# One GpSimd subtraction a step handed to VectorE in the first attention half of an attention-and-experts layer

## What is computed

```python
disp = (x @ W_disp).reshape(B, T, nh, bd).transpose(0, 2, 1, 3)      # 16 heads of 16
disp_win = _windows(disp, delta)                                     # the last 64 positions
strain = disp_win - disp[:, :, :, None, :]
bond_act = gelu(strain @ W_strain + rel_emb @ W_pos)
bond_logits = (bond_act @ W_bond)[..., 0]
damage_act = gelu(strain @ W_dmg + b_dmg)
damage = sigmoid((damage_act @ W_dmg_out)[..., 0] + b_dmg_out[0])
logits = bond_logits - 10.0 * damage
weights = softmax(where(cmask, logits, -inf))                        # over the 64 positions
out = einsum('bntd,bntde->bnte', weights, val_win) ... @ W_cproj
```

## Time and profile before

| | |
|---|---|
| time, median of 3 runs | 3710.76 us (3703.95 to 3714.79) |
| the profiled execution | 3708.35 us, its span 3706.8 us |
| busy over the span | DVE 77%, ACT 67%, PE 67%, POOL 63%, PEld 33% |
| first attention half, 350 to 1660 us | ACT 1096.7, DVE 1090.1, POOL 1022.6, PE 890.8 us busy |

### The profile page before, as it was taken

One profiled execution on the slowest core, in us unless ns is written; L12 is line 12 of the kernel. 1 busy time (PEld: TensorE's weight loads), 2 busy tenths in 40 slices (PEclk: granted clock), 3 DMA queues, 4 the chain that ended last, 5 costly groups with the idle time before them and its releaser, 6 DMA issues. The chain is left out here.

```text
span 3706.8 us, 64220 instructions
## 1 busy us (share of the span) xinstructions
PE 2501.0 (67%) x21226; PEld 1211.9 (33%) x21226; DVE 2861.7 (77%) x4254; ACT 2500.9 (67%) x1716; POOL 2327.2 (63%) x1604
## 2 busy tenths in 40 slices
PE   4662666776676766767888885566666676667666
PEld 2441112222222222246666661122222222222224
DVE  6888988888888888822433337999999899989981
ACT  1111979988888888843333337878878877778883
POOL 1222888678787878823343437777777777667771
PEclk9886879888888898868999997878778877878885
DMA  6773122222222222226878872222222222222222
GB/s 247 284 277 129 38 78 84 90 88 85 68 86 86 84 97 76 77 89 195 243 243 244 242 241 74 70 78 73 81 70 84 71 82 76 75 82 78 77 69 88
DMA packets 366243, 435.33 MB, mean 117 GB/s; under 512 B 48673, under 2 KB 282993, under 8 KB 366066
## 3 DMA queue, kind: packets, MB, share of 16 engines
q1 hardware_dynamic: 284658, 278.53, 24.0%
q0 software_dynamic: 57216, 143.22, 11.6%
q10 hardware_dynamic: 24192, 11.02, 1.1%
HBM read 233.83 MB, written 198.77 MB: 117 GB/s over the span
## 5 line engine op out<-in xcount | busy, mean ns | idle before, releaser
L1069 DVE SCALAR_TENSOR_TENSOR u_dve<-s_win,rpos,ps_here 128x512 f32<-128x512 f32 x1792 | 1197.6, 740 | 213.4 <-PE ps_l L1153 107.6
L1153 PE MATMUL ps_l<-u_dve,wsel 128*32 128x512 f32 x6144 | 984.8, 770 | 392.6 <-ACT u_dve L993 186.1
L927 POOL TENSOR_TENSOR u_pool<-s_win 128x4096 f32<-128x4096 f32 x128 | 1021.7, 7982 | 7.5 <-DMA s_win<-s_dram 5.3
L993 ACT ACTIVATE u_dve<-u_dve 128x4096 f32<-128x4096 f32 x224 | 809.9, 3616 | 56.8 <-DVE u_dve L1069 56.7
L1064 DVE TENSOR_TENSOR u_dve<-s_win,ps_here 128x4096 f32<-128x4096 f32 x160 | 703.3, 4412 | 43.1 <-PE ps_l L1153 43.1
L915 POOL DMA_INDIRECT yg<-yslot_dram,slot_now x512 | 485.6, 948 | 285.7 <-issue 148.5
L906 POOL DMA_INDIRECT xslot_dram<-xr,slot_now x512 | 494.6, 966 | 147.0 <-issue 143.6
L991 ACT ACTIVATE u_pool<-u_pool,bdmg_sb 128x4096 f32<-128x4096 f32 x128 | 474.5, 3707 | 66.1 <-POOL u_pool L927 66.1
L991 ACT ACTIVATE u_dve<-u_dve,bdmg_sb 128x4096 f32<-128x4096 f32 x128 | 474.4, 3706 | 15.8 <-DVE u_dve L1064 15.5
L1153 PEld LDWEIGHTS ps_l<-u_dve,wsel 128*32 128x32 f32 x6144 | 194.8, 128 | 842.8 <-issue 549.8
L1014 ACT ACTIVATE at_sb<-ps_u 128x512 f32<-128x512 f32 x256 | 151.0, 590 | 375.3 <-PE ps_u L1216 301.7
(11 more groups left out here) (142 smaller groups left out, 3011.1 us busy)
## 6 DMA issues: line engine op xcount, KB each, us to landing
band<-band_dram SPq DMA_DIRECT2D x32, 2048.0 KB
xslot_dram<-zero SPq DMA_DIRECT2D x16, 2688.0 KB, 9.1
xs<-xslot_dram SPq DMA_DIRECT2D x168, 256.0 KB, 3.6
yslot_dram<-ys POOLq DMA_DIRECT2D x168, 256.0 KB, 3.2
band_dram<-ml SPq DMA_DIRECT2D x64, 512.0 KB
we<-in_w_expert SPq DMA_DIRECT2D x336, 64.0 KB, 2.8
s_win<-s_dram SPq DMA_DIRECT2D x64, 288.0 KB, 5.9
s_dram<-s_sb POOLq DMA_DIRECT2D x16, 1024.0 KB, 4.7
```

Of the source, the lines that this page charges most:

```text
L927: pool.tensor_tensor(item_buffer(n), windows(par, ty, d0, 8), s_win[:, par, ty, PAD:PAD + TC].unsqueeze(1).to_broadcast([P, 8, TC]), ALU.s ...
L993: act.activation(u, u, ACT.Gelu).then_inc(gelu_done, 1)
L1069: last = dve.scalar_tensor_tensor(out=item_buffer(n)[:, d, :], in0=s_win[:, par, ty, d0 + d + 1:d0 + d + 1 + TC], scalar=rpos[:, d0 + d:d0 ...
L1153: last = pe.matmul(ps_l[32 * g:32 * g + 32, cgrp % 2, ty, :], wsel[:, ty, q, :], item_buffer(n)[:, d, :], start=(q == 0), stop=(q == 3))
```

## The change

In the first half VectorE subtracts the item n = 15 as well, 13 items a step, and GpSimd three (3, 7 and 11). The buffer of item 15 stays the one of `u_pool` in which GpSimd wrote it. The second half keeps its 12 and 4. The two semaphores' counts differ between the halves now, so that every wait on them in the second half is shifted by what the first left over (`D0`, `P0`). The subtraction of item 15 is the form that VectorE uses for `ty` 1 already (L1064), and it reads `ps_here`.

```diff
-            NP = len(on_pool)
-            dve_of = [sum(q % 4 not in on_pool for q in range(n + 1)) for n in range(NI)]
+            by_pool = ((3, 7, 11), (3, 7, 11, 15))[half]
+            dve_of = [sum(q not in by_pool for q in range(n + 1)) for n in range(NI)]
+            D0, P0 = ((0, 0), (first, -first))[half]
...
-                    return u_pool[:, (pool_of[n] - 1) % 2]
+                    return u_pool[:, n // 4 % 2]
...
-                    return n + 1 - 8 // NP
+                    return n - 7
...
-                            if "i" in st and n % 4 in on_pool:
+                            if "i" in st and n in by_pool:
                                 if pool_of[n] == 1:
                                     pool.wait_ge(win_loaded[par], 32 * it + 32)
...
-                                if n % 4 in on_pool:
-                                    if some(NPI * s + pool_of[n]):
-                                        act.wait_ge(sub_pool, NPI * s + pool_of[n])
+                                if n in by_pool:
+                                    if some(NPI * s + P0 + pool_of[n]):
+                                        act.wait_ge(sub_pool, NPI * s + P0 + pool_of[n])
...
-                            if "i" in st and n % 4 not in on_pool:
+                            if "i" in st and n not in by_pool:
...
-                        if some(ND * s):
-                            pe.wait_ge(sub_dve, ND * s)
+                        if some(ND * s + D0):
+                            pe.wait_ge(sub_dve, ND * s + D0)
```

More of the change, by code:

```diff
@@ L742, in load_windows @@
                         if some(it):
-                            if some(ND * (2 * it + par - 1)):
-                                sp.wait_ge(sub_dve, ND * (2 * it + par - 1))
+                            if some(ND * (2 * it + par - 1) + D0):
+                                sp.wait_ge(sub_dve, ND * (2 * it + par - 1) + D0)
                                 sp.sem_inc(held, 1)
-                            if some(NPI * (2 * it + par - 1)):
-                                sp.wait_ge(sub_pool, NPI * (2 * it + par - 1))
+                            if some(NPI * (2 * it + par - 1) + P0):
+                                sp.wait_ge(sub_pool, NPI * (2 * it + par - 1) + P0)
                                 sp.sem_inc(held, 1)
@@ L977, in step @@
                             if "i" in st:
-                                if n % 4 in on_pool:
-                                    if some(NPI * s + pool_of[n]):
-                                        act.wait_ge(sub_pool, NPI * s + pool_of[n])
-                                else:
-                                    if some(ND * s + dve_of[n]):
-                                        act.wait_ge(sub_dve, ND * s + dve_of[n])
+                                if n in by_pool:
+                                    if some(NPI * s + P0 + pool_of[n]):
+                                        act.wait_ge(sub_pool, NPI * s + P0 + pool_of[n])
+                                else:
+                                    if some(ND * s + D0 + dve_of[n]):
+                                        act.wait_ge(sub_dve, ND * s + D0 + dve_of[n])
                                 u = item_buffer(n)
```

## The result

The changed kernel takes 3742.07 us in the median of 5 runs (3736.60 to 3746.78), the kernel before 3710.76 us beside it (5 runs, 3703.95 to 3714.79): 1.0085 times as long, 95% interval 1.0069 to 1.0101, so 31 us slower. (The table ahead gives the same median and range for the kernel before as of 3 runs; they are of these 5.) The forecast was 3754 us, in a range of 3716 to 3780.

The account below looks back on a forecast made before the run. No engine is full; a chain of waits through ScalarE, TensorE and VectorE bounds the first half. 5.4 + 4.3 + 21 + 13.2 = 43.9 us on 3708.35 us gives 3752.3, stated as 3754 us, range 3716 to 3780.

Parts of the forecast that it names:

- GpSimd's relief, 0: First half: one GpSimd subtraction fewer a step, 7.98 us, gains 0 on the path; at most 43.6 us.
- The chain through `here`: At step changes TensorE's `here` starts 4.3 us later and takes 3.78 us at the lower clock, delaying work queued behind.
- The odd steps, 3.0 us each, 21 in all: Seven changes into steps 3 to 15: item 13 late, ScalarE loses 3.0 us each, between 0.5 and 4.4.
- the even steps, 2.2 each, 13.2 in all: Six changes into steps 4 to 14: item 13 3.9 us late, partly given back; between 0.5 and 3.9 us each.
- The first two changes, 9.7 us: Steps 0 to 1 and 1 to 2, where VectorE is the bound: 5.4 us and 4.3 us.
- The second half, unchanged: The second attention half was to stay as it was in the trace after.
- Hidden: Rival: VectorE's pauses take the work, only the first two changes cost, 9 us; 3720 us or less; chance 0.13.
- Full price: Rival: 4.3 us and the slow `here` passed on at all 15 step changes, 92 us, 3800 us; chance 0.12.

Follow-up runs that it names:

- the relief alone: Kernel before, but in the first half nobody subtracts item 15, so GpSimd has 3 items and VectorE its old 12: 3708.71 us for 3706.08, 1.0003.
- the wait without any work: Kernel before, no subtraction moved, but TensorE's `here` in the first half also waits for GpSimd's item 15: 3731.99 us for 3707.68, 1.0070.
- the work is 2.3 us: Changed kernel, but VectorE subtracts only 4 of item 15's 8 distances, the others left out: 3706.04 us, 0.9997 to the kernel before.
- `here` is free: Changed kernel, but VectorE's item 15 reads the row from `s_win`, so `here` waits only for item 14: 3713.34 us, 1.0020 to the kernel before.
- the second 4.4 us: Changed kernel, but VectorE does item 15's subtraction twice, 8.8 us: 3818.27 us for 3704.50 of the kernel before, 1.0309.
- The kernel with item 3: Changed kernel, but VectorE takes item 3 from GpSimd instead of item 15, `here` untouched: 3741.39 us, 1.0090 to the kernel before.
- taking `here` out of TensorE's way: Changed kernel, with first-half `here` moved behind turn 4 and values 2 of n = 12: 3728.89 us, 1.0065 to the kernel before.

## Why the prediction held, and where its sizes were off

**GpSimd's relief, 0.** Right, shown by itself: 1.0003 with the relief alone. GpSimd's idle time ahead of `spread` and `y_sb` took the relief up. The relief itself was 7.33 us a step: the 7.98 of the forecast were the mean of all four items. Groups of POOL in the kernel after, 430 to 1640 us (the kernel before had 65.6 us ahead of the first and 18.3 ahead of the second):

```profile
L896 POOL COPY v_one<-v_raw 128x1024 f32<-128x1024 f32 x7 | 7.3, 1046 | 116.7 <-PE ps_o L1127 100.8 <-issue 15.9
L940 POOL TENSOR_TENSOR y_sb<-y_sb,part_t 128x512 f32<-128x512 f32 x6 | 7.7, 1284 | 75.3 <-ACT y_sb L1025 75.3
```

51.1 us more in 7 steps is 7.3 us each, and 57.0 in 6 is 9.5: the forecast was about 8.

**The chain through `here`.** Right in its mechanism behind the first steps: `here` late by 4.4 us and at the lower clock (3.4 to 3.8 us at every change), the copy at n = 14 waiting 2.2 to 2.9 us from the change 2 to 3 on, and the wait without any work costing 26 us. VectorE's wait that ends with `here` is 38.6 us in 10 long ones, 3.9 us each, as foreseen; 4 more of the same length, 15.4 us, stand in the view under "issue".

**The odd steps, 3.0 us each, 21 in all; the even steps, 2.2 each, 13.2 in all.** By the exponents the odd came to 17.6 (2.2, 3.4, 1.8, 3.5, 2.7, 3.9 and 0.1), the even to 8.9 (2.8, 2.9, -2.3, 1.7, 1.8 and 2.0), together 26.5 for 34.2. This is the term of the sum that was mis-sized, and the clock says a good part of why. I had read one change of each kind and multiplied. The lengths of items 13 and 14 at all thirteen changes part them in another way. In the kernel before, one of the two is a long one (3.1 to 3.6 us) at ten changes, and both at three: into step 8, which I took as the pattern of the even ones, into step 12 and into step 15. The timeline of the kernel before at the change into 12:

```profile
1280.90 3.64 PE L1153 MATMUL ps_l<-u_dve,wsel 128*32 128x512 f32 x16 [3.26 <-ACT u_dve L991]
...
1286.48 3.64 PE L1153 MATMUL ps_l<-u_dve,wsel 128*32 128x512 f32 x16
```

and of the kernel after at the same one:

```profile
1310.08 1.92 PE L1154 MATMUL ps_l<-u_dve,wsel 128*32 128x512 f32 x16
1314.41 1.92 PE L1154 MATMUL ps_l<-u_dve,wsel 128*32 128x512 f32 x16 [1.20 <-ACT u_dve L994]
```

In the kernel after both are short at all thirteen: the slow stretch lies at `here` and is over behind it. Where the kernel before had two long items, the change cost -2.3, 1.8 and 0.1 us, nothing on the average; at the ten others 26.9 us, 2.7 each, against 2.6 in the forecast's mean. In the working of the even steps a faster item 13 and a faster item 14 gave back 1.7 us each; I took the first alone, 2.2 us, and with both, the lower end of 0.5, it would have met these three on the average. I never counted how often two long items stood there.

Three changes are few, and the -2.3 into step 8 has another cause beside them: TensorE's pause at the jump, which the forecast took from this change, was 4.72 us there, but 3.50, 3.86 and 3.10 into steps 6, 10 and 12, and 3.41 to 3.52 at all four in the kernel after. The kernel with the relief alone is 2.7 us shorter into step 8 too. It is a second reference, for TensorE's and VectorE's work stands in it as in the kernel before, and it has two long items at eight of the thirteen changes (into 3, 4, 8, 9, 10, 13, 14 and 15). Against it the kernel after loses 7.6 us at these eight, 1.0 each, and 12.5 at the five others, 2.5 each. So the reading holds: where two slow items stood already, a slow `here` in their place costs less. How many there are differs between these two executions, 3 and 8; what decides it is open.

**The first two changes, 9.7 us.** They came to 3.9 and 3.3, 7.2 us. The wait alone cost nothing there (-1.3 us), but in that kernel `here` wasn't late yet; how much is VectorE's load and how much `here` was not separated.

**The second half, unchanged.** Right within 2.3 us. I did not look for the origin of these.

**The rivals.** Hidden (3720 us or less) is what happens when the work is 2.3 us, or when `here` is free (1.0020): cover exists, and the change's 4.4 us go beyond it. Full price is what the second 4.4 us cost. The full price of the first, 92 us, was not paid. The kernel with item 3 shows what my account lacked: it put the cost on TensorE's order alone, while VectorE's way to `ml` is nearly as tight, since taking `here` out of TensorE's way recovered only some 7 us.

## What to carry to other kernels

Where no engine is full, work that is moved from one engine to another is priced by what waits for its last instruction, not by the two busy times; here the relieved engine gave back nothing, and one late wait of another engine cost 26 us by itself, for the 31 of the whole change. Measure the wait and the work apart (wait added without the work, work added without the wait): the two gave 26 and 7 us. Look in the trace whether the instruction still takes as long in its new form, though: here three of sixteen took nearly twice as long. And when a wait at one of two nearly equal chains is taken away, look at the other before counting the gain: each time, half or all of it turned up there.

## What the runs showed that I had not expected

While VectorE subtracts with both inputs in SBUF, a scatter issued by GpSimd takes up to five times as long, and the two engines' subtractions exclude each other. In the kernel with `here` free, where item 15 reads `s_win` twice instead of `s_win` and `ps_here`, the timeline of the change from 6 to 7 has

```profile
883.19 0.97 POOL L907 DMA_INDIRECT xslot_dram<-xr,slot_now  x1 [0.30 <-issue]
...
884.46 5.09 POOL L907 DMA_INDIRECT xslot_dram<-xr,slot_now  x1 [0.30 <-issue]
889.86 0.97 POOL L907 DMA_INDIRECT xslot_dram<-xr,slot_now  x1 [0.30 <-issue]
```

The long one starts 0.16 us after VectorE's subtraction (884.30, 4.41 us) and ends 0.84 us after it. Over the half, 13 of 478 scatters took 4.2 to 5.2 us, one beside each of 13 items 15. In the kernel after, where the same subtraction has one of its inputs in PSUM, the longest of 475 is 1007 ns. VectorE's subtraction keeps its 4.41 us beside a scatter that starts later.

With GpSimd's subtraction, the one that starts later is held up. In step 0 VectorE was first (415.02, 4.41 us):

```profile
415.69 11.84 POOL L928 TENSOR_TENSOR u_pool<-s_win 128x4096 f32<-128x4096 f32 x1
```

That is 8.2 us counted from about the end of VectorE's. In steps 1, 2 and 3 GpSimd was first, and VectorE's took 7.91 to 8.20 us, ending 4.3 to 5.3 us behind GpSimd's. In the kernel after, VectorE's item 15 of step 2 (571.33) runs beside a subtraction of GpSimd (566.81, 8.20 us) and takes 4.42 us. The Trainium skill (SBUF — State Buffer, SBUF: two separate sides) says that a VectorE instruction with two SBUF inputs and a GpSimd instruction that reads SBUF exclude each other for the whole length of an instruction, and that the first to start has its way; these lengths agree with that, and the scatter behaves as such an instruction. Behind step 4 the long scatters cost this kernel nothing that can be measured (-1.4 us over 11 changes).
